# Eight-core attention and ternary FFN: staging loads moved from the POOL queue to the SP queue, and the scaling of o moved from ScalarE to VectorE

## The chip, the cores and the metric

The kernel runs on all 8 cores of one Trainium2 chip, each core on its own 1024 rows of a sequence of 8192, with no communication between them. The metric is the device time of the slowest core, in microseconds (us). It is a median over executions; the profile is of one further execution.

## The reference

One layer, pre-norm: attention with a sliding window of 1024, then a feed-forward step with ternary inputs and weights. Cut to what is computed:

```python
def _layernorm(x): m = mean(x); v = mean((x - m)**2); return (x - m) / sqrt(v + 1e-5)
# attention, 16 heads of 128, over x of 8192 x 2048
h = _layernorm(x)
q, k, v = split(h @ Wqkv, 3)                      # Wqkv 2048 x 6144
q = rope(rmsnorm(q, q_norm_w)); k = rope(rmsnorm(k, k_norm_w))
scores = q @ k.T / sqrt(128)                      # per head
scores = where(q_idx >= k_idx and q_idx - k_idx <= 1023, scores, -inf)
x = x + (softmax(scores) @ v) @ Wo                # Wo 2048 x 2048
# feed-forward
xq = ternary(_layernorm(x), 0.33, 0.5)            # +-0.5 or 0
wq = ternary(weight, 0.2, 0.6) + rram_variation   # 2048 x 2048
x = x + xq @ wq.T
```

## The kernel before

Each core holds its own 1024 rows and the 1024 before them, 16 tiles `t` of 128 rows. The program is written out by hand as one instruction stream per engine (`Plan.op`, `Plan.wait`, `Plan.dma`), in stages that end with a barrier (`p.run`): P0 loads constants, P1 does the first norm and transposes, P2 computes k, P3 q, P4 v (spilled to DRAM), P5 attention, P6 the product with Wo and the residual, P7 the second norm and the ternary step, P8 the feed-forward product and the stores of y. Every engine runs its stream in order, and a wait holds everything behind it on that engine. The engines SP (`sync`) and POOL (`gpsimd`) do nothing here but issue DMAs, each from its own stream, after the waits that stand before them; POOL runs a few small fills at the start beside that. `Plan.dma` (line 118 through `Plan.op`) is the line of all DMAs in the profile.

*Weight chunks (P2, P3, P4 in `qkv_pass`, P6 in its own loop).* A product goes through chunks `ci` of 512 columns of the weight. A chunk is 16 blocks `d` of 128 x 512, cast to bf16 into `wchunk`, which exists once. So VectorE waits for the last matmul of the chunk before (`prev_mm`), casts 16 blocks, and TensorE waits for the last cast. The blocks come through two staging buffers of 256 KB: even `d` through `wstgA`, loaded by SP, odd `d` through `wstgB`, loaded by POOL. Each load waits until the cast of the block before it in that buffer has ended (`stg_guard`, a counter `cv` of VectorE); the casts run in the order of `d`, so A and B alternate. The first two loads of a chunk wait only for the last two casts of the chunk before, and for what stands ahead of them in the queue. In P4, POOL has the spills of v (`vhbm`) ahead of them, in P6 the loads of x for the residual (`x_all` into `xres`). Then, per tile, 16 matmuls accumulate in `psA` or `psB` and ScalarE or VectorE takes the result out (lines 398, 407, 726, 733).

*Attention (P5).* For each tile `j` of 128 queries: a first pass over the 16 heads for the row maxima (lines 573 and 577), then for each head `h` the functions `emit_ST(h)` and `emit_PV(h-1)`. `emit_ST` makes 18 matmuls for the transposed scores of 9 key blocks (lines 619, 624), ScalarE takes their exponential into `PTb` (line 632), and VectorE multiplies the first and the last block with masks (lines 637, 640). `emit_PV` makes 9 matmuls of the probabilities with v and 9 with a column of ones, both into the single buffer `psC` (lines 653, 659); VectorE takes the reciprocal of the sum (line 665), ScalarE scales and writes o into `R1` (line 670), and the next `emit_PV` waits for that (`psc_guard`).

*Feed-forward (P8).* The same chunks, but a block is built from two loads of 256 KB: `wfT` (SP) and `rrT` (POOL), each with two staging buffers (`wstgA` and a half of `ropeo`; `wstgB` and the other half). ScalarE takes two signs of `wfT` (lines 822, 824), VectorE adds them (828) and adds `rrT` scaled (833, `built_guard`). After each tile VectorE adds the residual into `sa` (line 854) and POOL stores it to y; `sa` is single, so each waits for the store before. The loads of `rrT` of the next chunk come after the stores of y in POOL's stream.

Of the kernel before, what the change touches and what calls it, by code (L numbers as in the profile page):

```python
# [8 lines left out]
AF = mybir.ActivationFunctionType  # L9
# [6 lines left out]
NH = 16  # L16
# [120 lines left out]
def build_nc(kphases=99, p1lvl=4):  # L137
    nc = bass.Bass("TRN2", target_bir_lowering=False)
# [3 lines left out]
    wo_d = nc.dram_tensor("wo", [D, D], F32, kind="ExternalInput").ap()  # L142
    wfT_d = nc.dram_tensor("wfT", [D, D], F32, kind="ExternalInput").ap()
    rrT_d = nc.dram_tensor("rrT", [D, D], F32, kind="ExternalInput").ap()
# [18 lines left out]
    R1 = sba("R1", [128, 34816], BF16)  # L163
# [59 lines left out]
    RNG = Ctr(nc, "rng")  # L223
    XR = [Ctr(nc, "xr0"), Ctr(nc, "xr1"), Ctr(nc, "xr2"), Ctr(nc, "xr3")]
    dO = Ctr(nc, "dO")
    WG0 = Ctr(nc, "wG0")
    WG1 = Ctr(nc, "wG1")
    ct = Ctr(nc, "ct")
    cv = Ctr(nc, "cv")
    cs = Ctr(nc, "cs")  # L230
# [131 lines left out]
    def qkv_pass(pl, col0, nchunks, tiles, dst_fn, pre_evac=None, post_evac=None,  # L362
                 w_dram=None, lhs_col=None):
        if w_dram is None:
            w_dram = wqkv_d
        if lhs_col is None:
            lhs_col = lambda t, d: 128 * (16 * t + d)
        ev = {}
        stg_guard = [None, None]
        par_guard = [None, None]  # L370
        prev_mm = None
        for ci in range(nchunks):
            c0 = col0 + 512 * ci
            if prev_mm is not None:
                pl.wait("vector", ct, prev_mm)
            for d in range(16):
                si = d % 2
                stg = wstgA if si == 0 else wstgB
                qeng = "sync" if si == 0 else "gpsimd"
                qsem = WS[0] if si == 0 else WG0  # L380
                if stg_guard[si] is not None:
                    pl.wait(qeng, cv, stg_guard[si])
                ld = pl.dma(qeng, stg[:], w_dram[128 * d:128 * (d + 1), c0:c0 + 512],
                            qsem)
                pl.wait("vector", qsem, ld)
                dstw = wchunk[:, 512 * d:512 * (d + 1)]
                stg_guard[si] = pl.op("vector", lambda e, s=stg, w=dstw: e.tensor_copy(  # L387
                    out=w, in_=s), ins=[stg[:]], out=dstw, sem=cv)
            cast15 = stg_guard[1]
            pl.wait("tensor", cv, cast15)  # L390
            for ti, t in enumerate(tiles):
                par = ti % 2
                ps = (psA if par == 0 else psB)[:, 0:512]
                if par_guard[par] is not None:
                    pl.wait("tensor", cs, par_guard[par])
                ctm = None
                for d in range(16):
# [12 lines left out]
                if post_evac is not None:  # L410
                    post_evac(pl, t, ci, ev[(t, ci)])
            prev_mm = ctm
        return ev
# [141 lines left out]
    for j in range(NQ):  # L555
# [47 lines left out]
        nm2_prev = nm2  # L603
        p.wait("tensor", RNG, ring_ld[j + 8])
        mk_of = {}

        def emit_ST(h):
            par = h % 2
# [20 lines left out]
            if pt_guard[par] is not None:  # L629
# [3 lines left out]
                out=PT, in_=ps[:, 0:1152], func=AF.Exp), ins=[ps[:, 0:1152]], out=PT,  # L633
                sem=cs)
            bank_guard[par] = (cs, expv)
            p.wait("vector", cs, expv)
            p.op("vector", lambda e, PT=PT: e.tensor_mul(  # L637
                PT[:, 0:128], PT[:, 0:128], masks[:, 0:128]),
                ins=[PT[:, 0:128]], out=PT[:, 0:128])
            mk_of[h] = p.op("vector", lambda e, PT=PT: e.tensor_mul(  # L640
                PT[:, 1024:1152], PT[:, 1024:1152], masks[:, 128:256]),
                ins=[PT[:, 1024:1152]], out=PT[:, 1024:1152], sem=cv)

        def emit_PV(h):
            nonlocal psc_guard
# [1 line left out]
            PT = PTb[:, 1152 * par:1152 * (par + 1)]  # L647
            p.wait("tensor", cv, mk_of[h])
            if psc_guard is not None:
                p.wait("tensor", cs, psc_guard)  # L650
            for l in range(NKT):
                sl = (j + l) % NKT
                p.op("tensor", lambda e, PT=PT, l=l, sl=sl, h=h: e.matmul(  # L653
# [4 lines left out]
            for l in range(NKT):  # L658
# [3 lines left out]
                    sem=(ct if l == NKT - 1 else None))  # L662
            pt_guard[par] = (ct, ctpv)
            p.wait("vector", ct, ctpv)
            rcv = p.op("vector", lambda e, h=h: e.reciprocal(
                rinv[:, h:h + 1], psC[:, 128:129]), ins=[psC[:, 128:129]],
                out=rinv[:, h:h + 1], sem=cv)
            p.wait("scalar", cv, rcv)
            oc = o_col(j, h)
            psc_guard = p.op("scalar", lambda e, h=h, oc=oc: e.activation(  # L670
                out=R1[:, oc:oc + 128], in_=psC[:, 0:128], func=AF.Copy,
                scale=rinv[:, h:h + 1]), ins=[psC[:, 0:128], rinv[:, h:h + 1]],
                out=R1[:, oc:oc + 128], sem=cs)

        emit_ST(0)
        for h in range(1, NH):
            emit_ST(h)
            emit_PV(h - 1)
# [18 lines left out]
    for ci in range(4):  # L697
# [3 lines left out]
        for d in range(16):  # L701
            si = d % 2
            stg = wstgA if si == 0 else wstgB
            qeng = "sync" if si == 0 else "gpsimd"
            qsem = WS[0] if si == 0 else WG0
            if stg_guard6[si] is not None:
                p.wait(qeng, cv, stg_guard6[si])
            ld = p.dma(qeng, stg[:], wo_d[128 * d:128 * (d + 1), c0:c0 + 512], qsem)
            p.wait("vector", qsem, ld)
            dstw = wchunk[:, 512 * d:512 * (d + 1)]  # L710
            stg_guard6[si] = p.op("vector", lambda e, s=stg, w=dstw: e.tensor_copy(  # L711
                out=w, in_=s), ins=[stg[:]], out=dstw, sem=cv)
# [93 lines left out]
    for ci in range(4):  # L806
# [2 lines left out]
            p.wait("vector", ct, prev_mm8)  # L809
        for d in range(16):  # L810
            si = d % 2
            rsem = WG0 if si == 0 else WG1
            if built_guard[si] is not None:
                p.wait("sync", cv, built_guard[si])
                p.wait("gpsimd", cv, built_guard[si])
                p.wait("scalar", cv, built_guard[si])
            ldw = p.dma("sync", stgW[si][:], wfT_d[128 * d:128 * (d + 1), c0:c0 + 512],
                        WS[si])
            ldr = p.dma("gpsimd", stgR[si][:], rrT_d[128 * d:128 * (d + 1), c0:c0 + 512],
                        rsem)  # L820
            p.wait("scalar", WS[si], ldw)
            p.op("scalar", lambda e, s=stgW[si], tA=tmpA[si]: e.activation(  # L822
                out=tA, in_=s[:], func=AF.Sign, bias=-0.2), ins=[stgW[si][:]], out=tmpA[si])
# [3 lines left out]
            p.wait("vector", cs, sgn)  # L827
            p.op("vector", lambda e, tA=tmpA[si], tB=tmpB[si]: e.tensor_add(tA, tA, tB),  # L828
                 ins=[tmpA[si], tmpB[si]], out=tmpA[si])
            p.wait("vector", rsem, ldr)  # L830
            dstw = wchunk[:, 512 * d:512 * (d + 1)]
            built_guard[si] = p.op(
                "vector", lambda e, s=stgR[si], w=dstw, tA=tmpA[si]: e.scalar_tensor_tensor(  # L833
# [25 lines left out]
            out_guard = p.dma("gpsimd", y_d[128 * j:128 * (j + 1), c0:c0 + 512],  # L859
                              outstg[:, 0:512], dO)  # L860
        prev_mm8 = ctm
    for cc in [dO, RNG, dC, SP[0], SP[1], WG0, WG1] + XR:
        p.streams["gpsimd"].append(lambda e, s=cc.sem, v=cc.v: e.wait_ge(s, v))
    for cc in WS:
        p.streams["sync"].append(lambda e, s=cc.sem, v=cc.v: e.wait_ge(s, v))
# [54 lines left out]
```

## Time and profile before

| | us |
|---|---|
| median of 2 runs | 3436.3 (3435.6 to 3437.0) |
| profiled execution, whole | 3409.8 |
| its span on the slowest core (core 4) | 3408.0 |
| spans of the 8 cores | 3372.8 to 3408.0 |
| TensorE busy, share of the span | 54% |
| DMA queues, share of 16 engines: POOL's, SP's | 7.5%, 6.8% |

How to read the rows below. The first view gives, for a stretch in us from the span's start, its length and then the busy time of each engine with the number of instructions, in the order PE (TensorE matmul), PEld (TensorE weight load), DVE (VectorE), ACT (ScalarE), POOL, then the granted TensorE clock as a share of full speed, the mean busy share of the 16 DMA engines, and GB/s. In the view of the waits a row is: engine, tile and line that waited, what ended the wait, us in total, times, longest. In the timeline a row is: start, duration, engine, line, operation, output <- inputs, and in brackets the idle time before it and what ended it. An issue row gives the size of one DMA and the median time from issue to landing. SPq is SP's queue. L12 is line 12 of the kernel. Stages on core 4, in us: P1 to 273, P2 to about 911, P3 to 1315, P4 to 1717, P5 to 2624, P6 to 2906, P7 to 3044, P8 to the end.

### The profile page before, as it was taken

The numbers are of one execution on the slowest core, as the hardware profiler recorded it, in microseconds if no ns is written. First come the engines' busy times: TensorE is split into PE (matmuls) and PEld (weight loads), VectorE is DVE, ScalarE is ACT, GpSimd is POOL, SyncE is SP. The second block draws the span as 40 slices with busy tenths as digits, with TensorE's granted clock in tenths as the row PEclk, the third lists the DMA queues.
The fourth block names the chain that finished last, engine by engine and source line by source line (L and its number), as shares of the span: only waits on it lengthen the run. The fifth ranks groups of instructions, "written<-read, shape, count | busy, mean of one in ns | idle before, by whom it ended". The sixth has DMA issues, their size and how long they took to land. (4 is left out here: it accounts for less than half of the span.)

```text
span 3408.0 us, 30542 instructions; the slowest of 8 cores (3372.8 to 3408.0 us)
## 1 busy us (share of the span) xinstructions
PE 1851.2 (54%) x9517; PEld 886.2 (26%) x9600; DVE 643.9 (19%) x1300; ACT 864.2 (25%) x1696; POOL 184.3 (5%) x345
## 2 busy tenths in 40 slices
PE   1224665503235423566678998899888636213333
PEld 0111222201112101222234554455445212101111
DVE  0000000033210032000033213321331111222222
ACT  4761100543200242011012222222223200442221
POOL 0000000000000000111100000000000111001111
PEclk9999877755567755888755555555555667556666
DMA  3211111000121101211110000000000232013333
GB/s 100 74 62 56 50 50 44 0 0 1 34 71 50 43 0 54 67 58 59 56 59 7 7 1 7 7 7 1 7 7 26 78 108 87 0 41 119 118 115 101
DMA packets 60540, 156.23 MB, mean 46 GB/s; under 512 B 12992, under 2 KB 12992, under 8 KB 58080
## 3 DMA queue, kind: packets, MB, share of 16 engines
q0 software_dynamic: 26016, 84.02, 7.5%
q1 hardware_dynamic: 34368, 70.27, 6.8%
q8 instruction: 81, 1.33, 0.2%
q14 instruction: 75, 0.61, 0.1%
HBM read 137.47 MB, written 16.78 MB: 45 GB/s over the span
## 5 line engine op out<-in xcount | busy, mean ns | idle before, releaser
L398 PE MATMUL psA<-wchunk,R 128*128 128x512 bf16 x1253 | 311.7, 403 | 449.5 <-DVE wchunk L387 448.2
L244 PE MATMUL psD<-identb,ropeo 128*128 128x128 bf16 x320 | 84.4, 264 | 489.5 <-DVE ropeo L482 254.8
L398 PEld LDWEIGHTS psA<-wchunk,R 128*128 128x128 bf16 x1280 | 130.3, 102 | 619.2 <-issue 485.2
L398 PE MATMUL psB<-wchunk,R 128*128 128x512 bf16 x1254 | 287.5, 379 | 1.4
L846 PE MATMUL psA<-wchunk,R 128*128 128x512 bf16 x251 | 65.2, 416 | 229.2 <-DVE wchunk L833 228.8
L244 PEld LDWEIGHTS psD<-identb,ropeo 128*128 128x128 bf16 x320 | 33.5, 105 | 541.1 <-issue 541.1
L619 PE MATMUL psA<-R 128*128 128x128 bf16 x576 | 163.6, 284 | 9.9 <-ACT wstgB L599 9.9
L398 PEld LDWEIGHTS psB<-wchunk,R 128*128 128x128 bf16 x1280 | 125.2, 98 | 151.0
L619 PE MATMUL psB<-R 128*128 128x128 bf16 x576 | 163.8, 284 | 0.0
L248 ACT COPY R<-psD 128x128 bf16<-128x128 bf16 x384 | 101.8, 265 | 216.4 <-PE psC L244 128.0
L653 PE MATMUL psC<-R,PTb 128*128 128x128 bf16 x1152 | 145.6, 311 | 12.4 <-ACT R L670 12.4
L637 DVE TENSOR_TENSOR PTb<-PTb,masksb 128x128 bf16<-128x128 bf16 x128 | 28.8, 225 | 609.2 <-ACT PTb L632 609.2
L387 DVE CAST wchunk<-wstgA 128x512 bf16<-128x512 f32 x96 | 41.1, 428 | 527.9 <-PE psB L398 439.4
L118 POOL DMA_DIRECT2D wstgB<-wqkv x96 | 52.1, 543 | 1399.9 <-POOLq L130 773.4
L726 PE MATMUL psA<-wchunk,R 128*128 128x512 bf16 x251 | 66.7, 423 | 106.9 <-DVE wchunk L711 105.6
L653 PEld LDWEIGHTS psC<-R,PTb 128*128 128x128 bf16 x1152 | 112.1, 141 | 26.9 <-issue 12.9
L632 ACT ACTIVATE PTb<-psA 128x1152 bf16<-128x1152 f32 x64 | 72.3, 1130 | 183.3 <-PE psA L624 183.3
L407 ACT CAST R<-psA 128x512 bf16<-128x512 f32 x48 | 28.1, 585 | 351.9 <-PE psA L398 351.8
L632 ACT ACTIVATE PTb<-psB 128x1152 bf16<-128x1152 f32 x64 | 72.3, 1130 | 168.6 <-PE psB L624 168.6
L248 ACT COPY R<-psC 128x128 bf16<-128x128 bf16 x384 | 101.8, 265 | 37.9 <-PE psC L244 4.7
L577 DVE TENSOR_REDUCE nmaxs<-psA 128x1 f32<-128x1152 f32 x64 | 86.9, 1357 | 79.8 <-PE psA L573 74.1
L244 PE MATMUL psC<-identb,ropeo 128*128 128x128 bf16 x320 | 84.6, 264 | 27.2 <-ACT R L248 4.1
(118 smaller groups left out, 2352.1 us busy)
## 6 DMA issues: line engine op xcount, KB each, us to landing
wstgA<-wqkv SPq DMA_DIRECT2D x96, 256.0 KB, 3.2
wstgB<-wqkv POOLq DMA_DIRECT2D x96, 256.0 KB, 3.8
wchunk<-x_all SPq DMA_DIRECT2D x16, 1024.0 KB, 4.8
vhbm<-PTb POOLq DMA_DIRECT2D x64, 128.0 KB, 2.2
R<-vhbm POOLq DMA_DIRECT2D x16, 512.0 KB, 4.0
wstgA<-wo SPq DMA_DIRECT2D x32, 256.0 KB, 3.0
wstgB<-wo POOLq DMA_DIRECT2D x32, 256.0 KB, 3.5
R<-x_all POOLq DMA_DIRECT2D x32, 256.0 KB, 3.9
```

The source lines that it names most:

```text
L118: return self.op(eng, lambda e, d=dst, s=src: e.dma_start(out=d, in_=s), sem=ctr, n=16)
L244: tv = pl.op("tensor", lambda e, s=slot, x=src_ap: e.transpose(s, x, identb[:]), sem=ct)
L248: g = pl.op("scalar", lambda e, s=slot, dd=dst_ap: e.copy(dd, s), ins=[slot], out=dst_ap, sem=cs)
L387: stg_guard[si] = pl.op("vector", lambda e, s=stg, w=dstw: e.tensor_copy(out=w, in_=s), ins=[stg[:]], out=dstw, sem=cv)
L398: ctm = pl.op("tensor", lambda e, d=d, t=t, ps=ps: e.matmul(ps, xlnT[:, lhs_col(t, d):lhs_col(t, d) + 128], wchunk[:, 512 * d:512 * (d + 1 ...
L577: red[h] = p.op("vector", lambda e, ps=ps, h=h: e.tensor_reduce(out=nmaxs[:, h:h + 1], in_=ps[:, 0:1152], axis=AX.X, op=ALU.max, negate=Tr ...
L619: p.op("tensor", lambda e, ps=ps, l=l, kb=kbase, q=q_ap: e.matmul(ps[:, 128 * l:128 * (l + 1)], kT[:, kb + 128 * l:kb + 128 * (l + 1)], q, ...
L632: expv = p.op("scalar", lambda e, ps=ps, PT=PT: e.activation(out=PT, in_=ps[:, 0:1152], func=AF.Exp), ins=[ps[:, 0:1152]], out=PT, sem=cs)
L637: p.op("vector", lambda e, PT=PT: e.tensor_mul(PT[:, 0:128], PT[:, 0:128], masks[:, 0:128]), ins=[PT[:, 0:128]], out=PT[:, 0:128])
L653: p.op("tensor", lambda e, PT=PT, l=l, sl=sl, h=h: e.matmul(psC[:, 0:128], PT[:, 128 * l:128 * (l + 1)], vring[:, 2048 * sl + 128 * h:2048 ...
L726: ctm = p.op("tensor", lambda e, ps=ps, c0o=c0o, h=h: e.matmul(ps, R1[:, c0o:c0o + 128], wchunk[:, 512 * h:512 * (h + 1)], start=(h == 0), ...
L846: ctm = p.op("tensor", lambda e, ps=ps, c0x=c0x, d=d: e.matmul(ps, xqT[:, c0x:c0x + 128], wchunk[:, 512 * d:512 * (d + 1)], start=(d == 0) ...
```

## The change

Three edits. (1) In P2, P3, P4 and P6 the odd blocks are loaded by SP too, in the order of `d`, with semaphores of their own. (2) In P8 the loads of `rrT` go to SP, each right behind the load of `wfT` of the same block. POOL keeps the constants, the spills and reloads of v, the loads of x and the stores of y. (3) In P5 the scaling of o goes from ScalarE to VectorE, and VectorE's order becomes: reciprocal of head h, the two masks of head h+1, scaling of head h.

```diff
-                qeng = "sync" if si == 0 else "gpsimd"
-                qsem = WS[0] if si == 0 else WG0
                 if stg_guard[si] is not None:
-                    pl.wait(qeng, cv, stg_guard[si])
-                ld = pl.dma(qeng, stg[:], w_dram[128 * d:128 * (d + 1), c0:c0 + 512],
-                            qsem)
-                pl.wait("vector", qsem, ld)
+                    pl.wait("sync", cv, stg_guard[si])
+                ld = pl.dma("sync", stg[:], w_dram[128 * d:128 * (d + 1), c0:c0 + 512],
+                            WS[si])
+                pl.wait("vector", WS[si], ld)
...
+        def emit_masks(h):
+            PT = PTb[:, 1152 * (h % 2):1152 * (h % 2 + 1)]
+            p.wait("vector", cs, exp_of[h])
+            p.op("vector", lambda e, PT=PT: e.tensor_mul(
+                PT[:, 0:128], PT[:, 0:128], masks[:, 0:128]),
+                ins=[PT[:, 0:128]], out=PT[:, 0:128])
+            mk_of[h] = p.op("vector", lambda e, PT=PT: e.tensor_mul(
+                PT[:, 1024:1152], PT[:, 1024:1152], masks[:, 128:256]),
+                ins=[PT[:, 1024:1152]], out=PT[:, 1024:1152], sem=cv)
...
-            rcv = p.op("vector", lambda e, h=h: e.reciprocal(
+            p.op("vector", lambda e, h=h: e.reciprocal(
                 rinv[:, h:h + 1], psC[:, 128:129]), ins=[psC[:, 128:129]],
-                out=rinv[:, h:h + 1], sem=cv)
-            p.wait("scalar", cv, rcv)
+                out=rinv[:, h:h + 1])
+            if h + 1 < NH:
+                emit_masks(h + 1)
             oc = o_col(j, h)
-            psc_guard = p.op("scalar", lambda e, h=h, oc=oc: e.activation(
-                out=R1[:, oc:oc + 128], in_=psC[:, 0:128], func=AF.Copy,
-                scale=rinv[:, h:h + 1]), ins=[psC[:, 0:128], rinv[:, h:h + 1]],
-                out=R1[:, oc:oc + 128], sem=cs)
+            psc_guard = p.op("vector", lambda e, h=h, oc=oc: e.tensor_scalar_mul(
+                R1[:, oc:oc + 128], psC[:, 0:128], rinv[:, h:h + 1]),
+                ins=[psC[:, 0:128], rinv[:, h:h + 1]],
+                out=R1[:, oc:oc + 128], sem=cv)
...
             if built_guard[si] is not None:
                 p.wait("sync", cv, built_guard[si])
-                p.wait("gpsimd", cv, built_guard[si])
                 p.wait("scalar", cv, built_guard[si])
...
-            ldr = p.dma("gpsimd", stgR[si][:], rrT_d[128 * d:128 * (d + 1), c0:c0 + 512],
-                        rsem)
+            ldr = p.dma("sync", stgR[si][:], rrT_d[128 * d:128 * (d + 1), c0:c0 + 512],
+                        WS[2 + si])
```

P6 changes as the first hunk does. The masks leave `emit_ST`; `emit_masks(0)` stands behind `emit_ST(0)`.

## Rows read from the trace of the kernel before

**Rows 1.** Busy time by stretch: P5, a staging pause of P2, one of P8.
```profile
1717.00:2624.00 907.00, 806.85 (x5112) 433.98 (x5120) 245.15 (x528) 208.93 (x273) 8.39 (x16) 0.51 0.03 10
...
457.00:491.00 34.00, 0.76 (x4) 0.14 (x2) 6.90 (x16) 0.58 (x1) 3.75 (x7) 0.58 0.39 116
...
3133.00:3187.00 54.00, 0.00 (x0) 0.00 (x0) 17.24 (x31) 17.62 (x28) 8.93 (x17) 0.50 0.56 156
```

**Rows 2.** Waits of TensorE for the last block of `wchunk`, whole span.
```profile
PE psA L398 <- DVE wchunk L387: 448.2, 12, 42.6
...
PE psA L846 <- DVE wchunk L833: 228.8, 4, 58.9
...
PE psA L726 <- DVE wchunk L711: 105.6, 3, 37.0
```

**Rows 3.** Timeline of VectorE and POOL in the first staging of P4.
```profile
1317.94 0.43 DVE L387 CAST wchunk<-wstgA 128x512 bf16<-128x512 f32 x1 [10.53 <-DMA wstgA<-wqkv]
...
1319.94 0.54 POOL L118 DMA_DIRECT2D wstgB<-wqkv  x1 [3.99 <-DVE wchunk L387]
...
1323.06 0.43 DVE L387 CAST wchunk<-wstgB 128x512 bf16<-128x512 f32 x1 [1.23 <-DMA wstgB<-wqkv]
...
1332.30 0.43 DVE L387 CAST wchunk<-wstgA 128x512 bf16<-128x512 f32 x1 [0.56 <-DMA wstgA<-wqkv]
...
1346.62 0.43 DVE L387 CAST wchunk<-wstgA 128x512 bf16<-128x512 f32 x1
1347.08 0.54 POOL L118 DMA_DIRECT2D wstgB<-wqkv  x1 [4.57 <-DVE wchunk L387]
1351.29 0.43 DVE L387 CAST wchunk<-wstgB 128x512 bf16<-128x512 f32 x1 [4.24 <-DMA wstgB<-wqkv]
```

**Rows 4.** DMA issues: queue, count, KB each, median us to landing.
```profile
wstgA<-wqkv SPq DMA_DIRECT2D x96, 256.0 KB, 3.2
wstgB<-wqkv POOLq DMA_DIRECT2D x96, 256.0 KB, 3.8
...
wstgA<-wfT SPq DMA_DIRECT2D x32, 256.0 KB, 3.0
```

**Rows 5.** Timeline at the start of P4's second chunk.
```profile
1411.44 0.54 POOL L118 DMA_DIRECT2D wstgB<-wqkv  x1
1415.12 0.43 DVE L387 CAST wchunk<-wstgB 128x512 bf16<-128x512 f32 x1 [4.86 <-DMA wstgB<-wqkv]
```

**Rows 6.** Timeline at the start of P8's second chunk.
```profile
3132.18 0.42 DVE L828 TENSOR_TENSOR PTb<-PTb 128x512 bf16<-128x512 bf16 x1
...
3140.25 0.69 DVE L833 SCALAR_TENSOR_TENSOR wchunk<-wstgB,PTb 128x512 bf16<-128x512 f32 x1 [7.66 <-DMA wstgB<-rrT]
...
3141.02 0.33 SPq L118 DMA_DIRECT2D wstgA<-wfT  x1
...
3142.55 0.33 SPq L118 DMA_DIRECT2D ropeo<-wfT  x1
...
3146.60 0.63 ACT L822 ACTIVATE PTb<-ropeo 128x512 bf16<-128x512 f32 x1 [0.33 <-DMA ropeo<-wfT]
```

**Rows 7.** Timeline of one head of P5, and TensorE's waits for `psC`.
```profile
1824.11 0.16 DVE L665 RECIPROCAL rinv<-psC 128x1 f32<-128x1 f32 x1
...
1824.42 0.37 ACT L670 ACTIVATE R<-psC,rinv 128x128 bf16<-128x128 f32 x1 [0.95 <-DVE rinv L665]
...
1827.16 1.14 PE L653 MATMUL psC<-R,PTb 128*128 128x128 bf16 x9
...
PE psC L653 <- ACT R L670: 12.4, 8, 1.9
```

**Rows 8.** Timeline of one staging pause of P2, first and last cast of B.
```profile
458.25 0.43 DVE L387 CAST wchunk<-wstgB 128x512 bf16<-128x512 f32 x1
...
490.03 0.43 DVE L387 CAST wchunk<-wstgB 128x512 bf16<-128x512 f32 x1 [4.36 <-DMA wstgB<-wqkv]
...
490.71 6.42 PE L398 MATMUL psA<-wchunk,R 128*128 128x512 bf16 x16 [33.24 <-DVE wchunk L387]
```

More of the change, by code:

```diff
@@ L225, in build_nc @@
     dO = Ctr(nc, "dO")
-    WG0 = Ctr(nc, "wG0")
-    WG1 = Ctr(nc, "wG1")
     ct = Ctr(nc, "ct")
@@ L605, in build_nc @@
         mk_of = {}
+        exp_of = {}
+        def emit_masks(h):
[7 more added lines that the diff above has]
+                ins=[PT[:, 1024:1152]], out=PT[:, 1024:1152], sem=cv)
         def emit_ST(h):
@@ L635, in emit_ST @@
             bank_guard[par] = (cs, expv)
[L636 to L642, printed above, removed]
+            exp_of[h] = expv
         def emit_PV(h):
@@ L649, in emit_PV @@
             if psc_guard is not None:
-                p.wait("tensor", cs, psc_guard)
+                p.wait("tensor", cv, psc_guard)
             for l in range(NKT):
@@ L664, in emit_PV @@
             p.wait("vector", ct, ctpv)
-            rcv = p.op("vector", lambda e, h=h: e.reciprocal(
+            p.op("vector", lambda e, h=h: e.reciprocal(
                 rinv[:, h:h + 1], psC[:, 128:129]), ins=[psC[:, 128:129]],
-                out=rinv[:, h:h + 1], sem=cv)
-            p.wait("scalar", cv, rcv)
+                out=rinv[:, h:h + 1])
+            if h + 1 < NH:
+                emit_masks(h + 1)
             oc = o_col(j, h)
-            psc_guard = p.op("scalar", lambda e, h=h, oc=oc: e.activation(
-                out=R1[:, oc:oc + 128], in_=psC[:, 0:128], func=AF.Copy,
-                scale=rinv[:, h:h + 1]), ins=[psC[:, 0:128], rinv[:, h:h + 1]],
-                out=R1[:, oc:oc + 128], sem=cs)
+            psc_guard = p.op("vector", lambda e, h=h, oc=oc: e.tensor_scalar_mul(
+                R1[:, oc:oc + 128], psC[:, 0:128], rinv[:, h:h + 1]),
+                ins=[psC[:, 0:128], rinv[:, h:h + 1]],
+                out=R1[:, oc:oc + 128], sem=cv)
         emit_ST(0)
+        emit_masks(0)
         for h in range(1, NH):
@@ L703, in build_nc @@
             stg = wstgA if si == 0 else wstgB
-            qeng = "sync" if si == 0 else "gpsimd"
-            qsem = WS[0] if si == 0 else WG0
             if stg_guard6[si] is not None:
-                p.wait(qeng, cv, stg_guard6[si])
-            ld = p.dma(qeng, stg[:], wo_d[128 * d:128 * (d + 1), c0:c0 + 512], qsem)
-            p.wait("vector", qsem, ld)
+                p.wait("sync", cv, stg_guard6[si])
+            ld = p.dma("sync", stg[:], wo_d[128 * d:128 * (d + 1), c0:c0 + 512], WS[si])
+            p.wait("vector", WS[si], ld)
             dstw = wchunk[:, 512 * d:512 * (d + 1)]
@@ L811, in build_nc @@
             si = d % 2
-            rsem = WG0 if si == 0 else WG1
             if built_guard[si] is not None:
                 p.wait("sync", cv, built_guard[si])
-                p.wait("gpsimd", cv, built_guard[si])
                 p.wait("scalar", cv, built_guard[si])
@@ L829, in build_nc @@
                  ins=[tmpA[si], tmpB[si]], out=tmpA[si])
-            p.wait("vector", rsem, ldr)
+            p.wait("vector", WS[2 + si], ldr)
             dstw = wchunk[:, 512 * d:512 * (d + 1)]
@@ L861, in build_nc @@
         prev_mm8 = ctm
-    for cc in [dO, RNG, dC, SP[0], SP[1], WG0, WG1] + XR:
+    for cc in [dO, RNG, dC, SP[0], SP[1]] + XR:
         p.streams["gpsimd"].append(lambda e, s=cc.sem, v=cc.v: e.wait_ge(s, v))
```

## Prediction

> **What bounds the kernel now.** I read four views. First the busy time by stretch [rows 1]: TensorE is busy 807 of 907 us in attention (P5, 1717 to 2624), and for 1 us of 34 while P2 stages a weight chunk. So two regimes alternate: matmuls, and pauses in which nothing but staging runs. Then TensorE's waits [rows 2]: in P2 to P4 it stands 448.2 us in 12 pauses until the last cast of `wchunk`, in P6 105.6 us in 3 (the fourth chunk is staged behind the transposes of o), in P8 228.8 us in 4. That is 782.6 us of the 3408, all of it serial, because `wchunk` is single. Third, the timeline of one pause in P4 [rows 3], for what paces it. Last, the lines around a chunk's end in P4 and P8 [rows 5, 6] and a head of attention [rows 7], with one whole pause of P2 [rows 8].
>
> Inside a pause two loops run side by side, slot A (SP) and slot B (POOL): load 256 KB, cast, load again; the casts alternate A, B on VectorE. Slot A goes from cast to cast in (1332.30 - 1317.94) / 4 = 3.59 us while it runs free. Slot B needs (1351.29 - 1323.06) / 6 = 4.70 us [rows 3]. The slower loop sets the pace, since A's next cast stands behind B's in VectorE's program. The medians to landing say the same: 3.2 us from SP, 3.8 us from POOL [rows 4]. SP starts its issue about 0.08 us after its slot's last VectorE operation (P8: 3140.25 + 0.69 to 3141.02) [rows 6]; POOL's issues come later, and that is in B's 4.70.
>
> The pause as a formula, from a pause of P2 [rows 8]: TensorE stood 33.24 us; from the first cast of B at 458.25 to the last at 490.03 are 31.78 us, seven steps of c = 4.54; what is left, 1.46 us, is the way from the last matmul to the first casts and from the last cast to the next matmul. So a chunk whose first two loads wait in staging already takes 1.46 us + 7c. For the first chunk of P2, P3 and P4 comes a landing more (3.2) and some 0.4 for the change of stage, an estimate: 5.1 + 7c, or 38.0 us with c = 4.70.
>
> **The change, part by part.**
>
> *Slot B and the second load of P8 go from POOL to SP.* B's loop becomes A's: cast 0.43, about 0.08 to the issue, landing 3.2, in sum 3.7; measured for A 3.59. SP now issues two loads per step of P2 to P6 and four in P8. P8 has 8 pairs in each of 4 pauses of together 228.8 us [rows 2], some 6 to 7 us a pair, and room for four issues of 0.33 us [rows 6]. POOL keeps the spills, the loads of x and v and the stores of y; in those queues nothing waits longer than before, it only has fewer things ahead of it.
>
> What can go wrong is that both loads share the 16 DMA engines. In rows 1 the stretch of the pause moved 116 GB/s at a share of 0.39, so at full share 297 GB/s, and 256 KB take 0.88 us of all engines. In rows 3 a POOL load with A's load between the casts lands so that the cast starts 3.12 us after the issue (1319.94 to 1323.06), one that is issued right behind A's 4.21 us (1347.08 to 1351.29), 1.1 us more, about one transfer of the other slot. So c is at best 3.5 (A alone, a little under its mean), at worst 3.6 + 0.9 = 4.5 (the second always behind the first). After the first step the two slots are 0.9 us apart, and then neither disturbs the other; but casts must alternate, so the later of two uneven landings counts each time. I take **c = 3.9**, a third of the way up, nearer the free row.
>
> The Trainium skill, SBUF — State Buffer, section "SBUF: two separate sides", says that a VectorE copy from float32 in a two-port mode locks GpSimd out of the port through which it writes the descriptors of its own DMAs, and that loads issued from SP are free of this. By it B's surplus is a lock, leaves with POOL altogether, and with c = 3.6 the sum below would be 31 us larger. The trace does not bear it out as the cause: A's cast ended at 1347.05 before POOL issued at 1347.08, and the load was late all the same [rows 3].
>
> Sum for 15 pauses: before 448.2 + 105.6 = 553.8 us [rows 2]. After: 12 x (1.46 + 27.3) = 345.1, and 3 x (5.1 + 27.3) = 97.2, together 442.3. Gain **111.5 us**. It should be largest in P4, where POOL can issue B's first load of a chunk only behind the last spill (at 1411.44, and cast B waited 4.86 us) [rows 5]; from there on both slots run in step, the bad phase. On SP it is issued as soon as its slot is free, half a hundred us earlier.
>
> *P8.* The loop of a slot runs over wfT: landing 3.0 [rows 4], two signs on ScalarE, add and build on VectorE, next load; rrT lands within it, hidden. So the steps stay at 6 us, whoever issues rrT. What goes is the start of chunks 2 to 4: VectorE had its add at 3132.18 and could build 0.57 later, at 3132.75, but rrT's load stood behind the last store of y on POOL, and the build came at 3140.25 [rows 6]. That is 7.5 us; I measured the same distance at the two other starts as 5.4 and 7.1. Gain **20 us**. If rrT in the same queue delays wfT of the other slot by 0.6 us a step (0.88 less their distance), 7 x 4 x 0.6 = 17 us of it are lost; if the missing mix of the two helps wfT, as much is won.
>
> *P5: o is scaled on VectorE, masks after the reciprocal.* Removed from ScalarE: 128 activations of 0.37 us. Added on VectorE: 128 scalings of 128 columns out of PSUM, not in the trace; the nearest row is ScalarE's own scaling of the same columns, 0.37 [rows 7], and I take that, with 0.16 (this engine on one column, the reciprocal) as the lower bound [rows 7] and 0.69 (this engine on 512 columns) as the upper [rows 6]. All of it lies under the next head's score matmuls: the scaling ended at 1824.79, the matmul that overwrites `psC` began at 1827.16 [rows 7], 2.4 us later, and TensorE never waited there. In the new order the same four operations follow each other, and the end moves by less than 0.5 us. The mask of head h+1 now stands behind head h's reciprocal, which waits for TensorE; but the probabilities are needed only after the next 18 score matmuls, so nothing queued behind it is late. Without that cover it would cost 0.37 us x 128 = 47 us. Open is the last head of a tile, where no score matmuls stand between: TensorE waited 12.4 us in 8 times [rows 7]. New chain: reciprocal, masks, scaling, against masks, reciprocal, a hop to ScalarE and its 0.37: 0.1 us shorter by my count, at most 0.3 either way, +-2.4 us in all. I take **0**.
>
> Total 111.5 + 20 = 131.5 us. The profiled execution took 3409.8 us (span 3408.0), the median of the runs is 3436.3; I subtract from the median: **3305 us**, 3.8% less.
>
> **Rivals.**
>
> 1. *Interference stays.* c = 4.5: the 15 pauses take 63 us more than in my sum, 3368 us, 2% faster. For it: in rows 3 the later steps ran at 4.7 to 5, with the slots in step. Against: that came from POOL's late start, which leaves; A's free steps of 3.59 were made with B's loads in flight.
>
> The Trainium skill, DMA: Bandwidth & Descriptors, section "Latency and other measured facts", has HBM latency rise under load, from 0.2 to 2 us; the pause would then lengthen the landings as it gets denser. The trace does not bear this out as far as it goes: in P8 156 GB/s moved [rows 1] at a median landing of 3.0 us [rows 4], and my pauses would move 4 MB in 29 us, 146 GB/s.
>
> 2. *No interference, c = 3.6.* 7 x 0.3 x 15 = 31 us better, 3274. For it: A ran at 3.59 beside B's loads. Against it: casts must alternate, so an uneven landing of either slot holds both. The lock that the Trainium skill describes (SBUF — State Buffer, as above) would also come out here.
>
> 3. *SP's loads run one after another (slower).* If SP's queue started a load only when the one before has landed, a step would be two landings, 6.4 us: 12 pauses of 46.3 and 3 of 49.9, 705 us against 554, and P8's four loads 12 us a step against 6, 28 steps x 6 = 168 us more. Some 3436 + 151 + 168 - 20 = 3735 us. It decides from c = 5 on, where the pauses are as long as before. Against it, [rows 6]: SP issued wfT at 3141.02 and again at 3142.55, and ScalarE read the second at 3146.60, 5.6 us after the first issue, in a phase with two POOL loads beside them; two landings in series would be 6 us and more.
>
> 4. *The clock.* After the pause of 33.24 us the first 16 matmuls took 6.42 us [rows 8], where 16 x 512 columns at the upper level (2.4 GHz) are 3.4 us: the granted clock, 0.58 in that stretch [rows 1], had fallen to its lower level (1.2 GHz). If pauses of 29 us kept the upper one, 16 starts would give back 2 us each, 32 us more, about 3273. In P8 and P2 alike the clock was near the lower level by the pause's mean, 0.50 and 0.58 [rows 1]; nothing there says that 29 us differ from 33.
>
> **How the numbers follow.** Forecast, c between 3.7 and 4.3: 0.60, 3284 to 3347. Rival 2 or 4: 0.18, 3250 to 3284. Rival 1: 0.17, around 3368. Rival 3: 0.04. A P8 that loses 17 us is inside these. The range 3250 to 3365 leaves out half of rival 1, rival 3 and the far ends. Two per cent, about what a measurement of this kernel can tell from none, is 3368: faster 0.60 + 0.18 + half of 0.17 = 0.86; same 0.10; slower 0.04.
>
> **What would show it.** Right: VectorE's casts of both slots 3.6 to 4.2 us apart; no `POOL wstgB` issue left; TensorE's waits for `wchunk` near 345 and 97 us in P2 to P6 and 209 in P8; P4's pauses as short as P2's; P5 within 3 us of 907. Wrong: landings from SP near 4 us in the median (rival 1); casts of A and B 3 us apart from each other at every step and steps over 6 (rival 3); TensorE waiting for `PTb` or `psC` inside a tile of P5; the first P8 build of a chunk still 5 us behind the add.

## The result and the profile after

| | before | after |
|---|---|---|
| median, us | 3419.6 (10 runs, 3396.9 to 3437.0) | 3254.8 (11 runs, 3245.0 to 3275.7) |
| profiled execution, us | 3409.8 | 3272.4 |
| span of its slowest core | 3408.0 (core 4) | 3270.5 (core 2) |
| TensorE's waits for the last block, P2 to P6, 15 pauses | 553.8 | 421.0 |
| the same in P8, 4 pauses | 228.8 | 213.7 |

In some executions of any of these kernels one die shows a lower granted clock and the time is 1% to 4% longer; such executions are left out of the comparisons below.

The ratio of the runs is 0.953, with a 95% interval of 0.949 to 0.956: 161 us less (165 between the medians), where 131.5 were forecast. The time lies in the range of 3250 to 3365 us, but only 5 us above its lower end: below the forecast of 3305, and below the 3284 down to which "c between 3.7 and 4.3" had been taken as the likely case.

The profile after, slowest core. First TensorE's waits (us in total, times, longest); the first four rows answer to [rows 2], the fifth to the waits for `psC` in [rows 7].

```profile
PE psA L394 <- DVE wchunk L383: 333.6, 12, 30.9
...
PE psA L845 <- DVE wchunk L832: 159.1, 3, 55.4
PE psA L727 <- DVE wchunk L712: 87.4, 3, 29.7
...
PE psA L845 <- ACT PTb L821: 54.6, 1, 54.6
...
PE psC L654 <- DVE R L672: 9.9, 8, 1.2
```

The same waits of P2 to P6 on core 4, the core of the rows before:

```profile
PE psA L394 <- DVE wchunk L383: 332.8, 12, 31.3
...
PE psA L727 <- DVE wchunk L712: 81.6, 3, 28.4
```

Of the rows of core 2, the fourth is the remaining pause of P8, only put down to another releaser. So P2 to P6 stand 333.6 + 87.4 = 421.0 us, P8 159.1 + 54.6 = 213.7.

The DMA issues (count, KB each, median us to landing), which answer to [rows 4]:

```profile
wstgA<-wqkv SPq DMA_DIRECT2D x96, 256.0 KB, 2.8
wstgB<-wqkv SPq DMA_DIRECT2D x96, 256.0 KB, 2.9
...
wstgA<-wfT SPq DMA_DIRECT2D x32, 256.0 KB, 3.1
wstgB<-rrT SPq DMA_DIRECT2D x32, 256.0 KB, 3.6
ropeo<-wfT SPq DMA_DIRECT2D x32, 256.0 KB, 3.3
```

Slot A's own load, which nobody touched, lands in 2.8 instead of 3.2 us. The experiments below show that it was slower because a load of POOL was beside it.

The timeline of a pause in P4 (core 2; start, duration, engine, line, operation, what it waited for), which answers to [rows 3, 5]:

```profile
1342.42 0.43 DVE L383 CAST wchunk<-wstgA 128x512 bf16<-128x512 f32 x1 [65.17 <-PE psB L394]
1342.92 0.33 SPq L118 DMA_DIRECT2D wstgA<-wqkv  x1
1342.95 0.43 DVE L383 CAST wchunk<-wstgB 128x512 bf16<-128x512 f32 x1
...
1346.82 0.33 SPq L118 DMA_DIRECT2D wstgA<-wqkv  x1
...
1347.46 0.33 SPq L118 DMA_DIRECT2D wstgB<-wqkv  x1
1349.67 0.43 DVE L383 CAST wchunk<-wstgA 128x512 bf16<-128x512 f32 x1 [2.28 <-DMA wstgA<-wqkv]
...
1350.37 0.43 DVE L383 CAST wchunk<-wstgB 128x512 bf16<-128x512 f32 x1 [0.27 <-DMA wstgB<-wqkv]
...
1367.06 0.43 DVE L383 CAST wchunk<-wstgA 128x512 bf16<-128x512 f32 x1 [1.45 <-DMA wstgA<-wqkv]
...
1368.63 0.43 DVE L383 CAST wchunk<-wstgB 128x512 bf16<-128x512 f32 x1 [1.14 <-DMA wstgB<-wqkv]
...
1369.31 3.14 PE L394 MATMUL psA<-wchunk,R 128*128 128x512 bf16 x7 [27.14 <-DVE wchunk L383]
```

The first cast of B stands right behind A's: its load had landed during the matmuls, where in [rows 5] it was issued only behind the last spill. Seven steps of A take (1367.06 - 1342.42) / 7 = 3.52 us, seven of B (1368.63 - 1342.95) / 7 = 3.67. With the second, the formula of the prediction gives 1.46 + 7 x 3.67 = 27.15 us, and TensorE stood 27.14. Note the two loads issued at 1346.82 and 1347.46, 0.64 us apart and so in each other's way if anything is: the casts follow 2.85 and 2.91 us after the issues, against the 4.21 us of a POOL load in [rows 3].

### The profile page after: what moved, and what is told of

The parts are those of the page before. It is cut to its first block and busy times, and to the rows that moved or that the text cites. A ratio compares the mean times of both kernels' runs of the same rounds, so it can differ in the third digit from the quotient of the medians.

```text
span 3270.5 us, 30245 instructions; the slowest of 8 cores (3230.1 to 3270.5 us)
## 1 busy us (share of the span) xinstructions
PE 1874.2 (57%) x9517; PEld 892.0 (27%) x9600; DVE 688.8 (21%) x1428; ACT 817.2 (25%) x1568; POOL 80.3 (2%) x153
## 5 line engine op out<-in xcount | busy, mean ns | idle before, releaser
L394 PE MATMUL psA<-wchunk,R 128*128 128x512 bf16 x1253 | 324.2, 414 | 335.1 <-DVE wchunk L383 333.6
L394 PE MATMUL psB<-wchunk,R 128*128 128x512 bf16 x1254 | 300.2, 391 | 1.6
L845 PE MATMUL psA<-wchunk,R 128*128 128x512 bf16 x251 | 64.8, 414 | 213.9 <-DVE wchunk L832 159.1
L666 DVE RECIPROCAL rinv<-psC 128x1 f32<-128x1 f32 x128 | 21.6, 168 | 497.9 <-PE psC L660 497.9
L727 PE MATMUL psA<-wchunk,R 128*128 128x512 bf16 x251 | 65.5, 417 | 88.6 <-DVE wchunk L712 87.4
L242 PE MATMUL psD<-identb,R 128*128 128x128 bf16 x128 | 33.9, 265 | 111.0 <-DVE R L786 86.5
```

The lines of the kernel that those rows point to most:

```text
L242: tv = pl.op("tensor", lambda e, s=slot, x=src_ap: e.transpose(s, x, identb[:]), sem=ct)
L394: ctm = pl.op("tensor", lambda e, d=d, t=t, ps=ps: e.matmul(ps, xlnT[:, lhs_col(t, d):lhs_col(t, d) + 128], wchunk[:, 512 * d:512 * (d + 1 ...
L727: ctm = p.op("tensor", lambda e, ps=ps, c0o=c0o, h=h: e.matmul(ps, R1[:, c0o:c0o + 128], wchunk[:, 512 * h:512 * (h + 1)], start=(h == 0), ...
L845: ctm = p.op("tensor", lambda e, ps=ps, c0x=c0x, d=d: e.matmul(ps, xqT[:, c0x:c0x + 128], wchunk[:, 512 * d:512 * (d + 1)], start=(d == 0) ...
```

## The experiments

To compare runs whose pauses have different lengths I use one number, c, the step of the slower slot, by the prediction's formula. Of the twelve pauses of P2 to P4 nine take 1.46 + 7c and three 5.1 + 7c, together 28.4 + 84c. Before, (448.2 - 28.4) / 84 = 5.0; after, (333.6 - 28.4) / 84 = 3.63. That the formula's fixed parts hold in all of these kernels is an assumption; c carries what they miss, above all a late start of the loads. So the table further down gives beside c the step itself, read from the timelines.

### The loads of the weights alone

```diff
 # the kernel before, P2 to P4 and P6
-                qeng = "sync" if si == 0 else "gpsimd"
-                qsem = WS[0] if si == 0 else WG0
...
-                ld = pl.dma(qeng, stg[:], w_dram[...], qsem)
+                ld = pl.dma("sync", stg[:], w_dram[...], WS[si])
```

> The kernel before with one part of the change alone: the odd weight blocks of P2, P3, P4 and P6 loaded by SP. Theory (staging on SP is nearly the whole gain): the 15 pauses fall from about 554 us to about 421 us as in the changed kernel, so 130 to 140 us less than before, a ratio near 0.960; P8's waits stay at 220 to 229 us. Rival (the edits help each other, for instance POOL's rrT loads in P8 or ScalarE's lighter load matter): under 110 us here, and the rest only with all three.

Measured: 3276.7 against 3406.8 us, ratio 0.961 (0.954 to 0.968). TensorE's waits (first two lines P2 to P4 and P6, the others P8):

```profile
PE psA L396 <- DVE wchunk L385: 333.3, 12, 30.5
PE psA L842 <- DVE wchunk L829: 174.9, 3, 59.5
...
PE psA L722 <- DVE wchunk L707: 86.3, 3, 29.8
PE psA L842 <- ACT PTb L818: 51.6, 1, 51.6
```

333.3 + 86.3 = 419.6 us: the whole gain of the 15 pauses is in this edit, 134 us, and the medians differ by 130. P8 stays as it was, 226.5 us.

### The loads of rrT alone

```diff
 # the kernel before, P8
-            ldr = p.dma("gpsimd", stgR[si][:], rrT_d[...], rsem)
+            ldr = p.dma("sync", stgR[si][:], rrT_d[...], WS[2 + si])
```

> The kernel before with the loads of rrT on SP alone. Theory: only the starts of chunks 2 to 4 of P8 get shorter, 15 to 20 us, ratio 0.994 to 0.996; P8's four pauses take 209 to 214 us instead of 221 to 229, and the steps inside a pause stay as long. Rival (rrT ahead of the next wfT in one queue lengthens each step): the pause's inner steps get longer by up to 0.6 us and the gain goes to zero.

Measured: 3394.2 against 3406.8 us, ratio 0.997 (0.994 to 1.001), not separable from no change. What VectorE waited for in P8, on core 4 in all three kernels: before,

```profile
DVE PTb L828 <- ACT PTb L824: 118.7, 58, 15.0
...
DVE wchunk L833 <- DMA wstgB<-rrT: 22.3, 5, 7.7
```

with this edit, and then in the full change,

```profile
DVE PTb L826 <- ACT PTb L822: 130.4, 58, 13.5
```

```profile
DVE PTb L827 <- ACT PTb L823: 124.4, 58, 13.6
```

The wait for `rrT`, 22.3 us, is gone as it should be. The wait for the signs, and so for `wfT`, grew by 11.7 us here and by 5.7 in the full change. The sums are -10.6 and -16.6; the pauses on core 4 went from 228.8 before to 221.9 here (6.9 less) and to 211.3 (155.2 + 56.1) after (17.5 less). `wfT` lands in 3.3 and 3.6 us (two slots) instead of 3.0 and 3.1. So the second load of a pair seems to cost the first load of the next slot something; here about half of the gain at the starts is given back, and the forecast of 15 to 20 us is missed. Why it costs twice as much here as in the full change I did not find; the cores of one execution differ by about that much (the kernel before has 221.4 us on core 2 and 228.8 on core 4).

The edit does one thing more, which was not forecast. The last store of y is issued, and the program ends, on core 4 before and in the full change:

```profile
3396.54 0.54 POOL L118 DMA_DIRECT2D y<-sa  x1 [3.24 <-DVE sa L854]
```

```profile
3231.37 0.54 POOL L118 DMA_DIRECT2D y<-sa  x1 [3.25 <-DVE sa L853]
```

From there to the end of the span (3408.0 and 3237.5) are 11.46 us before and 6.13 after. On the four cores that I read in each kernel (0, 2, 4, 6) it is 11.1 to 12.2 us in all five that load `rrT` from POOL, the one with the weights alone on SP among them, and 6.0 to 6.5 in all six that load it from SP, this one among them. So some 5.3 us of the end belong to the loads of `rrT` on POOL; why, the traces don't tell.

### The edit of P5 alone

```diff
 # the kernel before, P5
-            psc_guard = p.op("scalar", lambda e, ...: e.activation(out=R1[:, oc:oc + 128], ...))
+            psc_guard = p.op("vector", lambda e, ...: e.tensor_scalar_mul(R1[:, oc:oc + 128], ...))
 # and emit_masks(h + 1) between the reciprocal and the scaling
```

> The kernel before with the P5 edit alone (scaling of o on VectorE, masks after the reciprocal). Theory: hidden under the score matmuls, P5 changes by less than 3 us and the time by nothing measurable, ratio 0.999 to 1.001; TensorE's waits for psC about 10 us instead of 12.4. Rival (freeing ScalarE or the shorter chain matters): more than 5 us either way, and TensorE waits inside a tile.

Measured: 3397.0 against 3406.8 us, ratio 0.998 (0.995 to 1.002): nothing that can be seen. The group of the scaling, from the profile of the full change (busy us, mean ns of one, idle before):

```profile
L672 DVE TENSOR_SCALAR R<-psC,rinv 128x128 bf16<-128x128 f32 x128 | 44.2, 345 | 1.6 <-DVE rinv L666 0.8
```

345 ns, against ScalarE's 370 that the prediction took for it. TensorE's wait for `psC` at the last heads fell from 12.4 to 9.9 us, here as in the full change.

### B's loads of P2 to P4 issued by ScalarE

```diff
 # the changed kernel
-                    pl.wait("sync", cv, stg_guard[si])
-                ld = pl.dma("sync", stg[:], w_dram[...], WS[si])
+                    pl.wait("sync" if si == 0 else "scalar", cv, stg_guard[si])
+                ld = pl.dma("sync" if si == 0 else "scalar", stg[:], w_dram[...], WS[si])
```

> The changed kernel, but the odd blocks of P2 to P4 are loaded from ScalarE's queue, so A and B are issued by two engines and neither is POOL. Theory (what was slow is POOL as the issuer, not that two queues run at once): the steps inside a pause stay at 3.6 us, as with both on SP; the starts of later chunks get longer by a landing, 3 to 5 us, since ScalarE issues B's first load only after its last copy. Rival (two queues at once disturb each other, as A and B did in the kernel before): steps of 4.5 us and more in the same phase.

Measured: 3260.0 us, one execution. Waits of P2 to P4 345.0 us, c = 3.77. Its issues:

```profile
wstgA<-wqkv SPq DMA_DIRECT2D x96, 256.0 KB, 2.8
wstgB<-wqkv ACTq DMA_DIRECT2D x96, 256.0 KB, 2.8
```

Two loads in flight from two queues land as fast as two from one. The casts of A are 3.56 us apart in the mean and those of B 3.48, so the steps are no longer than in the changed kernel. What c has more, 3.77 against 3.63, is the start of a chunk (from a chunk's first cast to its last are 27.0 us in the mean instead of 25.9): ScalarE issues B's first load only after its last copy, as was expected. That the two slots were on different queues was no fault; that one of them was POOL's was.

### POOL without SP beside it: no loads of A

```diff
 # the kernel before, P2 to P4
+                if si == 1 or (ci == 0 and d == 0):
                     ld = pl.dma(qeng, stg[:], w_dram[...], qsem)
                     pl.wait("vector", qsem, ld)
```

> The kernel before, with B on POOL and A's loads left out in P2 to P4 (A's casts stay and read what is in the buffer, so the weights are wrong there). It separates what makes POOL's load about 0.8 us longer when it is issued right behind an A cast (4.1 us from issue to cast, against 3.3 otherwise). If A's load on the DMA engines is the cause: 3.1 to 3.3 us here, steps of 4.1 us, pauses of 30 us. If VectorE's cast just before, or POOL's own issue, is the cause: 4.1 us still, steps of 5 us, pauses of 36 to 37 us.

Measured: 3359.6 us, one execution. Waits of P2 to P4 384.5 us, c = 4.24, landings of POOL 2.9 us. Two steps of its timeline in P2, VectorE and POOL, core 2:

```profile
454.30 0.43 DVE L388 CAST wchunk<-wstgB 128x512 bf16<-128x512 f32 x1 [3.11 <-DMA wstgB<-wqkv]
454.83 0.43 DVE L388 CAST wchunk<-wstgA 128x512 bf16<-128x512 f32 x1
455.29 0.54 POOL L118 DMA_DIRECT2D wstgB<-wqkv  x1 [3.53 <-DVE wchunk L388]
458.57 0.43 DVE L388 CAST wchunk<-wstgB 128x512 bf16<-128x512 f32 x1 [3.31 <-DMA wstgB<-wqkv]
459.45 0.43 DVE L388 CAST wchunk<-wstgA 128x512 bf16<-128x512 f32 x1 [0.46 <-DVE wchunk L388]
459.55 0.54 POOL L118 DMA_DIRECT2D wstgB<-wqkv  x1 [3.73 <-DVE wchunk L388]
462.83 0.43 DVE L388 CAST wchunk<-wstgB 128x512 bf16<-128x512 f32 x1 [2.95 <-DMA wstgB<-wqkv]
```

The casts of A are all there, at the same place as before; only A's transfers are missing. B's cast now starts 3.28 us after the issue, 4.21 in [rows 3]. Over some 80 loads of P2 to P4 that a cast waited for, the median is 3.1 us here (core 3) and 4.0 in the kernel before (core 4). So what made B late was A's transfer beside it, and not VectorE. The third issue here bears on VectorE: it runs from 459.55 to 460.09, of which VectorE casts A until 459.88, and both its length (0.54) and the time to the next cast (3.28) are those of the issue at 455.29, which stands behind the cast of A. The Trainium skill, SBUF — State Buffer, section "SBUF: two separate sides", would have the cast hold up POOL's descriptors; these rows don't show it. Nor does the kernel before: there, on core 4, 14 issues of POOL overlap a cast of A and their load's cast starts 4.03 us after them in the median; the 66 that overlap none take 4.00.

What stays in c = 4.24 is POOL's own. POOL starts 0.55 to 0.56 us after the cast that frees the slot (454.73 to 455.29; 459.00 to 459.55), where SP starts 0.07 us after it (1342.85 to 1342.92 above).

### Both slots on POOL

```diff
 # the kernel before, P2 to P4
-                qeng = "sync" if si == 0 else "gpsimd"
-                qsem = WS[0] if si == 0 else WG0
+                qeng = "gpsimd"
+                qsem = WG1 if si == 0 else WG0
```

> The kernel before with both slots of P2 to P4 loaded by POOL. Theory (POOL as the issuer costs a late start of 0.55 us, an issue of 0.54 us and a longer landing): steps of 4.3 to 5.3 us, pauses no shorter than in the kernel before (31 to 43 us), so about the same time or up to 30 us slower. Rival (mixing two kinds of queue is what costs): with one kind alone the steps fall to 4.1 us or under, pauses near 30 us, and the kernel gains 50 us or more.

Measured: 3361.0 us, one execution; a second, 3416.8, is left out. Waits of P2 to P4 410.3 us, c = 4.55. Its issues:

```profile
wstgA<-wqkv POOLq DMA_DIRECT2D x96, 256.0 KB, 3.1
wstgB<-wqkv POOLq DMA_DIRECT2D x96, 256.0 KB, 3.1
```

Even with every load on the slower of the two queues the pauses are shorter than with one slot on each: 410.3 against 448.2 us. That is neither of the two expectations: the pauses should have stayed as long, or the steps should have fallen to 4.1 us. Together the five kernels split the step of the kernel before. The third column is the measured step of the slower slot, from its first to its last cast, the mean of eleven of the twelve pauses (the trace lacks records of the first):

| loads of A, B | c, us | measured step, us | landing A, B, us |
|---|---|---|---|
| SP, POOL (before) | 5.00 | 4.80 | 3.2, 3.8 |
| POOL, POOL | 4.55 | 4.32 | 3.1, 3.1 |
| none, POOL | 4.24 | 4.09 | -, 2.9 |
| SP, ScalarE | 3.77 | 3.56 | 2.8, 2.8 |
| SP, SP (after) | 3.63 | 3.62 | 2.8, 2.9 |

From the last row to the third, 0.61 us of c and 0.47 of the step, is POOL by itself: the later start accounts for the step. From the third to the first, 0.76 us of c and 0.71 of the step, is A's load on SP beside POOL's. A's load on POOL instead costs only 0.31 and 0.23, so some 0.45 us are the mixture, and with it that the casts wait for the later of two uneven landings. This rests on one execution of each of the three kernels in the middle. What inside the chip slows two such loads beside each other, these runs don't tell.

### Four slots in P2 to P6

```diff
 # the changed kernel; sa, sb: two buffers that are free in these stages
+    stg4 = [wstgA, wstgB, sa.bitcast(F32)[:, 0:512], sb_.bitcast(F32)[:, 0:512]]
...
-                si = d % 2
-                stg = wstgA if si == 0 else wstgB
+                si = d % 4
+                stg = stg4[si]
```

> The changed kernel with four staging buffers in place of two in P2, P3, P4 and P6, all loaded by SP (the two new ones are the buffers sa and sb, which are free there). Theory (a step is one landing plus a cast, so the pause is bound by latency, not by the data): a pair of blocks takes 1.8 to 2.4 us instead of 3.6, a prefetched pause 15 to 18 us instead of 27, some 140 to 170 us less than the changed kernel. Rival (the DMA engines are the bound, as my 0.88 us per 256 KB had it): a pair cannot take less than 1.8 us and with contention of eight cores stays above 3, less than 60 us gained. Beside that, with denser matmuls more stretches at a granted clock of 0.81 should be seen, as on one die of the changed kernel, if they come from matmul density; they would take back up to 30 us.

Measured: 3094.2 against 3416.2 us, ratio 0.907 (0.904 to 0.911). Waits and issues:

```profile
PE psA L395 <- DVE wchunk L384: 204.9, 12, 20.8
PE psA L728 <- DVE wchunk L713: 54.2, 3, 19.1
```

```profile
wstgA<-wqkv SPq DMA_DIRECT2D x48, 256.0 KB, 3.5
...
sa<-wqkv SPq DMA_DIRECT2D x48, 256.0 KB, 3.7
```

Twice the slots, and each load lands 0.7 to 0.8 us later. 259.1 us (204.9 + 54.2) of waits instead of 421.0. So after the change the pause was still latency, a round of landing, cast and issue for every second block, and the DMA engines had room: over the pause of P4 shown above, on core 2 from 1342 to 1370 us, they moved 145 GB/s at a share of 0.47.

### Four slots in P8 too

```diff
 # P8: four slots for wfT, four for rrT, in R1, which P8 does not read
-    stgW = [wstgA, ro2stgA[:, 0:512]]
-    stgR = [wstgB, ro2stgA[:, 512:1024]]
+    stgW = [R1f[:, 512 * i:512 * (i + 1)] for i in range(4)]
+    stgR = [R1f[:, 2048 + 512 * i:2048 + 512 * (i + 1)] for i in range(4)]
...
-            si = d % 2
+            si = d % 4
```

> The run with four staging slots in P2, P3, P4 and P6, and now four pairs of slots for wfT and rrT in P8 as well (the slots and the temporaries of the two signs lie in R1, which P8 does not read; all loads on SyncE's queue). Theory, that the wait of a staging step is the latency of its load, to be divided by the number of slots in flight: P8's pauses of 52 to 55 us, sixteen steps of about 3.3 us, fall towards the time in which SyncE issues and VectorE and ScalarE work, which is about 2 us for a step (two issues of 0.33 us and a pair of landings of at most 4 us over four slots on one side, one cast and one addition on the other), so 30 to 36 us a pause, waits in front of P8's first tiles about 130 instead of 217 us, and the time about 3010 to 3030 us (ratio to the kernel before 0.885). Rival, that SyncE's queue or the DMA engines are full in P8 with two tensors at once (512 KB a step): the landings of rrT rise from 3.7 to 6 us or more and the pauses stay above 45 us; the time stays above 3065 us.

Measured: 3044.8 against 3426.9 us, ratio 0.886 (0.881 to 0.892), the fastest kernel of this study. Waits of P8, its issues, and a pause by the busy time of each stretch (granted clock, DMA share and GB/s are the last three numbers):

```profile
PE psA L848 <- DVE wchunk L835: 112.9, 3, 41.7
...
PE psA L848 <- ACT PTb L826: 39.6, 1, 39.6
```

```profile
R<-wfT SPq DMA_DIRECT2D x64, 256.0 KB, 4.9
R<-rrT SPq DMA_DIRECT2D x64, 256.0 KB, 5.8
```

```profile
2749.00:2783.00 34.00, 0.52 (x2) 0.16 (x2) 14.50 (x26) 18.60 (x31) 0.00 (x0) 0.50 0.82 227
```

152.5 us of waits (112.9 + 39.6) instead of 217, so 38 us a pause, a little above the 30 to 36 of the theory, and the time 15 us above its upper end. The rival is half right: the landings of `wfT` rose from 3.1 to 3.3 us to 4.9, those of `rrT` from 3.6 to 3.7 us to 5.8, and the engines are busy to 0.82. Here the limit comes near to what the 16 engines carry. That another doubling would gain little is an estimate from the share of 0.82; no run tested it.

### The changed kernel once more

No edit.

> The changed kernel once more, unedited, for a second profile. The first profile showed stretches at a granted clock of 0.81 inside the dense matmuls, on cores 0 and 1 in P2 and on cores 2 and 3 in P4, and nowhere on cores 4 to 7; the profile of the kernel before has none longer than 5 us. Theory, that it is a passing state of one die in that execution: this profile shows no such stretch, or on other cores and in other stages, and its cores lie within 10 us of each other near 3235 to 3245 us. Rival, that the shorter pauses bring it on in the same place each time: cores 0 and 1 in 330 to 625 us and cores 2 and 3 in 1285 to 1585 us again, four stretches of 30 to 35 us each, those cores some 25 us behind cores 4 to 7. The waits for wchunk stay at 333 and 82 to 87 us in either case.

Measured: 3249.7 us, one execution, cores 3227.7 to 3247.8 us, waits 335.3, 90.3 and 213.7 us on core 2. The clock is told of in the last section.

## Why the prediction was right, and where it was not

**What bounds the kernel: right.** The pauses were serial time. The waits for `wchunk` fell by 132.8 us in P2 to P6 and by 15.1 in P8, together 147.9 between the two slowest cores, and the profiled execution by 137.4. The slowest core after, core 2, has stretches at a lower clock that cost some 25 us (last section). Core 4, which has none, is the cleaner pair: from 3408.0 to 3237.5 us, 170.5 less, with its waits down by 139.4 and 17.5. Of the 13.6 us that are left 5.3 are the shorter end of the program, 2.5 are `psC`, and 2.6 are one wait of TensorE at the start of P5 (10.0 us before, 7.4 after); some 3 us stay open.

**The step c: mis-sized, 3.9 where 3.63 to 3.70 was measured.** (421.0 - 32.8) / 105 = 3.70 us over the 15 pauses on core 2, (414.4 - 32.8) / 105 = 3.63 on core 4. That is rival 2, "no interference, c = 3.6", not the forecast. The failed step is "256 KB take 0.88 us of all engines", put beside the 4.21 us of [rows 3]: the one number explained the other, and so it was carried over to a slot that moves to SP. The runs show that the 4.21 us had another cause. Two loads 0.64 us apart on SP, or on SP and ScalarE, show no such surcharge; without A's transfers POOL's 4.21 becomes 3.28; so, in these stages, it belongs to a POOL load beside an SP load, and the change takes it away with the load itself. At a share of 0.39 or 0.47 the 16 engines had room in which a second load ran: four loads in flight landed only 0.7 to 0.8 us later than two.

**"POOL's issues come later, and that is in B's 4.70": right**, and worth 0.5 us of each step (0.55 us after the cast, SP 0.07).

**The lock: not the cause, as the prediction had read from rows 3.** It was right for a reason that one row could not carry; the run without A's loads, and the 14 overlapping issues against the 66 others, carry it.

**P4's pauses as short as P2's: right.** 27.1, 27.5 and 26.8 us in P4, 27.2, 27.0 and 26.1 in P2.

**P8: the starts right, the steps not.** In the second chunk, on core 4, the add at 2986.40 is followed by the build at 2986.96, where 7.5 us more lay between in [rows 6]; in the first chunk nothing was late before either. The wait for `rrT` of 22.3 us is gone, 20 were forecast. "So the steps stay at 6 us" failed by a little: `wfT` landed 0.1 to 0.2 us later in the median, and its waits grew by 5.7 us in sum; the prediction had it as a bound (17 us) and not in its sum. Net the pauses are 15.1 us shorter between the slowest cores and 17.5 on core 4, and 6.9 where this edit stands alone. The 5.3 us at the end of the program come on top and were not in the prediction.

```profile
2986.40 0.41 DVE L827 TENSOR_TENSOR PTb<-PTb 128x512 bf16<-128x512 bf16 x1
2986.96 0.69 DVE L832 SCALAR_TENSOR_TENSOR wchunk<-wstgB,PTb 128x512 bf16<-128x512 f32 x1
```

**P5: right.** 0 forecast, +-2.4; by the starts of the first score and the last `psC` matmul it takes 903.2 us on core 4 (1598.2 to 2501.4) where it took 905.6 (1717.0 to 2622.6).

```profile
L654 PE MATMUL psC<-R,PTb x1152: 263/314/314, 1637.0 to 2501.4; 128*128 128x128 bf16 x192
```

**The loads in series (rival 3): excluded.** With two loads in SP's queue a step is 3.5 to 3.7 us, not 6.4. **The clock (rival 4): no gain.** In the pause of P4 above the matmuls restart at the lower level as before: the first seven matmuls of 512 columns take 3.14 us, 0.45 us each. Over P2 to P4 on core 4 the matmuls into `psA`, the first of each pause among them, were busy for 312.5 us, and for 311.7 before. The price of the rival was also too low: in [rows 8] a start costs 6.42 - 3.4 = 3.0 us and not 2.

**The subtraction.** 131.5 us were taken from the median of two runs, 3436.3; ten runs of the kernel before have a median of 3419.6 and the profiled execution took 3409.8. From 3419.6 the same sum gives 3288. So of the 50 us between 3305 and 3254.8, 17 are that start and 33 a gain that was too small, most of it c (0.2 us x 105 = 21 us on core 2, 0.27 x 105 = 28 on core 4). Both errors point the same way. That the time still fell into the range is due to its lower part, which had been kept for rivals 2 and 4 and of which 5 us were left.

## What to carry to other kernels

When a transfer is late, ask first by whose queue it goes and what is beside it, and measure a load of the same size from the same queue alone, before the lateness is priced as shared bandwidth. Where a pause is a loop of load, convert and load again, its length is the latency of the load over the number of slots in flight: here the better queue was worth 161 us, and two slots more, which cost nothing but two idle buffers, another 160. Add slots until the landings rise as fast as their number. In P8, with eight loads in flight, the DMA engines were busy to 0.82.

## What the hardware showed that I had not expected

**POOL's and SP's loads slow each other in P2 to P4.** There 256 KB land in 2.8 us (SP beside SP or beside ScalarE) and in 2.9 (POOL alone), but in 3.2 and 3.8 with one of each. The Trainium skill, DMA: Bandwidth & Descriptors, section "Issuing engines are not separate DMA queues", has it that issuing from several engines only saves the time of the issue. For SP and ScalarE this case agrees (2.8 and 2.8 us); for POOL beside SP it doesn't, where A's load costs 0.76 us of c from SP and 0.31 from POOL. It is no general rule either. In P8, over all kernels with two pairs of slots there, `wfT` landed in 2.6 to 3.1 us with `rrT` on POOL and in 3.0 to 3.6 with `rrT` on SP, and `rrT` itself in 3.4 to 4.0 from POOL and 3.4 to 4.2 from SP: there no cost of the mixture shows. What sets the two stages apart was not tested.

**A third clock.** In the profile of the change, TensorE's dense matmuls ran for stretches of 30 to 40 us at a granted clock of 0.81, on cores 0 and 1 in P2 and on cores 2 and 3 in P4 (beside a few of at most 15 us elsewhere). The same 35 us in P4, on core 2 and then on core 4:

```profile
1285.00:1320.00 35.00, 34.73 (x132) 14.49 (x134) 0.00 (x0) 5.40 (x10) 4.87 (x9) 0.81 0.09 33
```

```profile
1285.00:1320.00 35.00, 34.84 (x161) 15.84 (x162) 0.00 (x0) 7.14 (x11) 5.41 (x10) 1.00 0.10 36
```

132 matmuls instead of 161 in the same time. Four such stretches, each some 30 matmuls of 0.22 us short, cost core 2 some 25 us, and the cores of its die have a median of 3261.3 us against 3235.2 for the other. In the second profile of the same kernel the same windows read 1.00, 0.99 and 1.00 on cores 2 and 4, and neither it nor the two kernels with four slots, whose pauses are shorter still, has a stretch longer than 10 us. So shorter pauses do not bring it on by themselves; what did in that execution stays open. The Trainium skill, TensorE: Matmul & The Clock Gate, section "Seeing it yourself", tells of a peak-current limit that takes a whole die to 13/16 of the clock while three of its cores run dense matmuls. The value agrees; that it takes a whole die for as long as its cores run dense matmuls is not seen here: the two pairs of cores had it in different stages, and cores 4 to 7 of the same execution, with the same work, stood at 1.00.
